# Query-key projection of a linear-attention and feed-forward block: seven block products per pair of tiles, with new engine orders

## The reference

```python
B, N, C, H = 8, 1024, 256, 16          # D = C // H = 16
xn = layernorm(x)                       # x: (8, 1024, 256) float32
qkv = xn @ qkv_w + qkv_b                # to (3, B, H, N, D)
q, k = l2norm(q), l2norm(k)             # over D
kv = einsum('bhnd,bhne->bhde', k, v)
attn = einsum('bhnd,bhde->bhne', q, kv).reshape(B, N, C) @ proj_w + proj_b
ffn = relu(xn @ W1 + b1) @ W2 + b2      # 256 -> 1024 -> 256
out = x + attn + ffn
```

## Time and profile before

| what | value |
|---|---|
| device time, three runs | 553.73, 553.97, 554.46 us (median 553.97) |
| span of the profiled execution, first to last instruction | 552.4 us |
| instructions | 8714 |
| TensorE busy, share of the span | 547.7 us, 99% |
| VectorE, ScalarE, GpSimd busy | 398.5, 286.9, 119.4 us |
| clock granted to TensorE | full speed throughout |

### The profile page before, as it was taken

One profiled execution on the slowest core, in us unless ns is written; L12 is line 12 of the kernel. 1 busy time (PEld: TensorE's weight loads), 2 busy tenths in 40 slices (PEclk: granted clock), 3 DMA queues, 4 the chain that ended last, 5 costly groups with the idle time before them and its releaser, 6 DMA issues.

```text
span 552.4 us, 8714 instructions
## 1 busy us (share of the span) xinstructions
PE 547.7 (99%) x2590; PEld 460.2 (83%) x2590; DVE 398.5 (72%) x791; ACT 286.9 (52%) x529; POOL 119.4 (22%) x150
## 2 busy tenths in 40 slices
PE   9999999999999999999999999999999999999997
PEld 7888888888888888888888888888888888888896
DVE  6977788567795876858667587775777767684655
ACT  4785654556336563465644556455553655533421
POOL 4242424202052020420213202331024201050100
PEclk9999999999999999999999999999999999999999
DMA  8522134343413434134341343315333251314312
GB/s 259 167 87 50 33 83 93 83 105 83 107 20 86 98 85 95 24 86 98 85 88 31 93 92 84 81 38 113 71 90 67 45 107 38 79 37 93 96 39 76
DMA packets 141413, 45.34 MB, mean 82 GB/s; under 512 B 133330, under 2 KB 136402, under 8 KB 141396
## 3 DMA queue, kind: packets, MB, share of 16 engines
q1 hardware_dynamic: 139280, 44.61, 34.7%
q10 hardware_dynamic: 2116, 0.53, 0.5%
HBM read 20.98 MB, written 8.39 MB: 53 GB/s over the span
## 4 chain that ended last, share of the span: by engine, by line
PE 99%; DVE 0%; issue 0%
PE o_bank L1169 12%; PE o_bank L1170 12%; PE o_bank L1171 12%; PE w_bank L1169 11%; PE w_bank L1170 11%; PE w_bank L1171 11%; PE v_bank L1169 7%; PE v_bank L1170 7%; PE v_bank L1171 7%; PE kv_bank L1307 3%; PE g_bank L1307 3%; PE kv_bank L1312 1%; PE g_bank L1312 1%; PE kv_bank L1323 1%; PE w_bank L1361 1%; PE g_bank L1171 0%
## 5 line engine op out<-in xcount | busy, mean ns | idle before, releaser
L957 DVE SCALAR_TENSOR_TENSOR h_lo<-w_bank,h_hi 128x512 fp32r<-128x512 f32 x128 | 87.4, 683 | 38.2 <-ACT h_hi L607 36.5
L607 ACT ACTIVATE h_hi<-w_bank 128x512 fp32r<-128x512 f32 x128 | 76.4, 597 | 66.5 <-PE w_bank L1171 66.4
L1169 PE MATMUL w_bank<-xT_hi,w_hi 128*128 128x512 f32 x254 | 99.9, 393 | 0.0
L1170 PE MATMUL w_bank<-xT_lo,w_hi 128*128 128x512 f32 x254 | 99.2, 391 | 0.0
L1171 PE MATMUL w_bank<-xT_hi,w_lo 128*128 128x512 f32 x254 | 98.9, 389 | 0.0
L1169 PE MATMUL o_bank<-h_hi,w_hi 128*128 128x512 f32 x240 | 93.5, 389 | 0.0
L1170 PE MATMUL o_bank<-h_lo,w_hi 128*128 128x512 f32 x240 | 93.4, 389 | 0.0
L1171 PE MATMUL o_bank<-h_hi,w_lo 128*128 128x512 f32 x240 | 93.4, 389 | 0.0
L405 POOL TENSOR_TENSOR xn_lo<-xn,xn_hi 128x256 fp32r<-128x256 f32 x56 | 42.5, 759 | 217.6 <-ACT xn_hi L517 213.4
L420 POOL TENSOR_TENSOR y_sb<-y_sb,y_rows 128x256 f32<-128x256 f32 x56 | 52.5, 941 | 123.7 <-DVE y_rows L1001 103.2
L585 ACT ACTIVATE qk_sq<-v_bank 128x512 f32<-128x512 f32 x64 | 38.3, 598 | 72.2 <-PE v_bank L1171 72.2
(11 more groups left out here) (213 smaller groups left out, 921.4 us busy)
## 6 DMA issues: line engine op xcount, KB each, us to landing
y_rows<-blocks SPq DMA_DIRECT2D x256, 32.0 KB, 1.9
x_sb<-x SPq DMA_DIRECT2D x15, 512.0 KB, 3.5
y_sb<-x SPq DMA_DIRECT2D x60, 128.0 KB, 3.3
out<-y_sb SPq DMA_DIRECT2D x58, 128.0 KB, 2.5
xT_raw<-blocks SPq DMA_DIRECT2D x224, 32.0 KB, 1.9
y_sb<-w SPq DMA_DIRECT2D x4, 256.0 KB, 5.1
x_sb<-x SPq DMA_DIRECT2D x2, 256.0 KB, 3.0
w_raw<-w SPq DMA_DIRECT2D x2, 256.0 KB, 7.4
```

The source lines that it names most:

```text
L607: nc.scalar.activation(h_hi[:, j % RING, :], w_bank[j % 2][:], ACT.Relu).then_inc(h_done, 1)
L957: nc.vector.scalar_tensor_tensor(h_lo[:, r, :], w_bank[j % 2][:], 0.0, h_hi[:, r, :].bitcast(F32), ALU.max, ALU.subtract).then_inc(h_lo_do ...
L1169: nc.tensor.matmul(to, left[0], right[0], start=first, stop=False, skip_group_check=shared)
L1170: nc.tensor.matmul(to, left[0], right[1], start=False, stop=False, skip_group_check=shared)
```

## The change

For the halves 3 to 15, the 512 x 256 by 256 x 512 query-key product is cut into blocks. A pair `n` (0 or 1) takes tiles `n` and `n + 2` as two block rows, the two channel chunks as the inner blocks, and the query and the key columns of the weight as two block columns. In place of eight block products (24 matmuls of 512 columns per half), seven are computed from sums and differences of blocks: 42 matmuls of 256 columns per half. The sums of the transposed input (`xf_raw`, four forms) are made by GpSimd (`x_forms`, one instruction of 512 elements per partition and two of 256), their high part by ScalarE (`x_forms_high`, 1024 elements) and their low part by VectorE (`x_forms_low`, 1024 elements). The sums of the weights are made once, by GpSimd (`weight_forms`). The shared partial results pass from one quarter of a bank to another between four bursts on TensorE: `qk_begin` (6 narrow matmuls), then ScalarE copies two quarters (`qk_seed`), `qk_second` (6), then VectorE adds (`qk_seed` of VectorE), `qk_third` (6), VectorE adds (`qk_sum`), `qk_fourth` (3). `xf_raw` lies in `xn`, and `wqk_forms` lies in `wvp_raw`, so that `normalise(s)` waits for `x_forms_low(s - 1)` and the first `yT_out(b, 1, ...)` waits for `weight_forms`. The core of the diff:

```diff
+X01_X00, X11_X01, X11_X01_X00, X10_X11_X01_X00 = range(FORMS)
+W_SIX, W_FIVE, W_FOUR, W_SEVEN = range(FORMS)
...
+        xf_raw = xn[:].rearrange("p t c -> p (t c)").rearrange("p (f n) -> p f n", f=FORMS)
+        wqk_forms = wvp_raw[:].rearrange("p w k n -> p (w k n)").rearrange("p (f n) -> p f n", f=FORMS)
...
+        qk_11, qk_22 = (v_bank[0][:, n * C:(n + 1) * C] for n in range(2))
+        qk_12, qk_21 = (v_bank[1][:, n * C:(n + 1) * C] for n in range(2))
...
+    def x_forms(s):
+        wait(pool, x_moved, 16 * MOVES * (s - 1))
+        first, second = slice(0, PAIR * P), slice(PAIR * P, HALF)
+        nc.gpsimd.tensor_tensor(xf_raw[:, 0:2], xT_raw[:, :, second],
+                                xT_raw[:, 0].rearrange("p (a n) -> p a n", a=PAIRS),
+                                ALU.subtract).then_inc(xf_sums_done, 1)
+        wait(pool, xf_sums_done, 2 * (s - FORMS_FROM) + 1)
+        nc.gpsimd.tensor_tensor(xf_raw[:, X11_X01_X00], xT_raw[:, 1, second], xf_raw[:, X01_X00],
+                                ALU.subtract).then_inc(xf_sums_done, 1)
+        wait(pool, xf_sums_done, 2 * (s - FORMS_FROM) + 2)
+        nc.gpsimd.tensor_tensor(xf_raw[:, X10_X11_X01_X00], xT_raw[:, 1, first], xf_raw[:, X11_X01_X00],
+                                ALU.subtract).then_inc(xf_raw_done, 1)
+    def weight_forms():
+        whole = wqk_forms.rearrange("p f n -> p (f n)")
+        pool.wait_ge(wvp_ready, 2)
+        nc.gpsimd.tensor_tensor(whole, wqk_hi[:].rearrange("p k n -> p (k n)").bitcast(F32),
+                                wqk_lo[:].rearrange("p k n -> p (k n)").bitcast(F32),
+                                ALU.add).then_inc(wqk_forms_summed, 1)
+        for n, (to, left, right, op) in enumerate(((W_SEVEN, 3, 1, ALU.add), (W_FIVE, 0, 1, ALU.subtract),
+                                                   (W_SIX, W_SEVEN, 0, ALU.subtract),
+                                                   (W_FOUR, 2, W_SIX, ALU.subtract))):
+            pool.wait_ge(wqk_forms_summed, n + 1)
+            nc.gpsimd.tensor_tensor(wqk_forms[:, to], wqk_forms[:, left], wqk_forms[:, right],
+                                    op).then_inc(wqk_forms_summed, 1)
+        pool.wait_ge(wqk_forms_summed, FORMS + 1)
+        nc.gpsimd.tensor_copy(wqk_forms_hi[:], wqk_forms).then_inc(wqk_forms_hi_ready, 1)
+        pool.wait_ge(wqk_forms_hi_ready, 1)
+        nc.gpsimd.tensor_tensor(wqk_forms_lo[:], wqk_forms, wqk_forms_hi[:].bitcast(F32),
+                                ALU.subtract).then_inc(wqk_forms_ready, 1)
...
+    def x_forms_high(s):
+        wait(act, xf_raw_done, s - FORMS_FROM + 1)
+        copy(xf_hi[:].rearrange("p f (b n) -> p f b n", b=PAIR),
+             xf_raw.rearrange("p f (n b) -> p f b n", b=PAIR)).then_inc(xf_hi_done, 1)
+    def qk_seed(s, n):
+        wait(act, qk_begun, pairs_done(s, n))
+        wait(act, qk_copied, TILES * s + 2 * n)
+        copy(qk_21, qk_11)
+        wait(act, qk_22_summed, pairs_done(s, n) - 1)
+        copy(qk_fifth[:], qk_22).then_inc(qk_seeded, 1)
+    def qk_pair_out(s, u, n, w):
+        if w == 0:
+            wait(act, qk_22_summed, pairs_done(s, n))
+        else:
+            wait(act, qk_21_done, pairs_done(s, n))
+        wait(act, qk_ss_done, TILES * s + 2 * n + w - 1)
+        nc.scalar.activation(qk_sq[:, w, :], v_bank[w][:], ACT.Square).then_inc(qk_sq_done, 1)
+        if n == 0 and w == 0:
+            wait(act, q_transposed, s - 1)
+            wait(act, k_lo_done, s - 1)
+        to = (off_diagonal if w else diagonal)(head_blocks(qk[u]), n)
+        copy(to, v_bank[w][:].rearrange("p (w n) -> p w n", w=2)).then_inc(qk_copied, 1)
...
+    def x_forms_low(s):
+        wait(dve, xf_hi_done, s - FORMS_FROM + 1)
+        less(xf_lo[:].rearrange("p f (b n) -> p f b n", b=PAIR),
+             xf_raw.rearrange("p f (n b) -> p f b n", b=PAIR),
+             xf_hi[:].rearrange("p f (b n) -> p f b n", b=PAIR)).then_inc(xf_lo_done, 1)
+    def qk_seed(s, n):
+        wait(dve, qk_21_sixth_in, pairs_done(s, n))
+        nc.vector.tensor_tensor(qk_12, qk_21, qk_fifth[:], ALU.add).then_inc(qk_12_seeded, 1)
+    def qk_sum(s, n):
+        wait(dve, qk_21_seventh_in, pairs_done(s, n))
+        nc.vector.tensor_tensor(qk_22, qk_21, qk_fifth[:], ALU.add).then_inc(qk_22_summed, 1)
...
+    def qk_begin(s, u, n, batch):
+        if n == 0 and u == 1:
+            wait(pe, yT_added, KC * batch)
+        if n == 0:
+            wait(pe, xT_hi_done, KC * (s + 1))
+            wait(pe, xT_lo_done, KC * (s + 1))
+        wait(pe, qk_copied, TILES * s + 2 * n - 1)
+        product(qk_11, (xT_hi[:, u, 0, tile(n)], xT_lo[:, u, 0, tile(n)]),
+                (wqk_hi[:, 0, 0:C], wqk_lo[:, 0, 0:C]), True, False, shared=True)
+        wait(pe, xf_lo_done, s - FORMS_FROM + 1)
+        qk_form(qk_22, X11_X01, w_form(W_FIVE), n).then_inc(qk_begun, 1)
+    def qk_form(to, x_form, weights, n):
+        hi, lo = weights
+        return product(to, (xf_hi[:, x_form, tile(n)], xf_lo[:, x_form, tile(n)]), (hi, lo), False, False,
+                       shared=True)
...
+    def qk_second(s, u, n):
+        wait(pe, qk_seeded, pairs_done(s, n))
+        qk_form(qk_21, X11_X01_X00, w_form(W_SIX), n).then_inc(qk_21_sixth_in, 1)
+        product(qk_11, (xT_hi[:, u, 1, tile(n)], xT_lo[:, u, 1, tile(n)]),
+                (wqk_hi[:, 1, 0:C], wqk_lo[:, 1, 0:C]), False, True, shared=True)
+    def qk_third(s, n):
+        wait(pe, qk_12_seeded, pairs_done(s, n))
+        qk_form(qk_12, X10_X11_X01_X00, (wqk_hi[:, 1, C:2 * C], wqk_lo[:, 1, C:2 * C]), n)
+        qk_form(qk_21, X01_X00, w_form(W_SEVEN), n).then_inc(qk_21_seventh_in, 1)
+    def qk_fourth(s, u, n):
+        wait(pe, qk_22_summed, pairs_done(s, n))
+        t = PAIR + n
+        product(qk_21, (xT_hi[:, u, 1, tile(t)], xT_lo[:, u, 1, tile(t)]), w_form(W_FOUR), False, True,
+                shared=True).then_inc(qk_21_done, 1)
```

More of the change, by code:

```diff
@@ L1080, in opening @@
                 divide(1, 1, k_done)
-            def half(b, s, u, last):
[L1083 to L1115, removed]
-                else:
[L1117 to L1136, removed]
-                if is_second(s):
-                    qT_low(s, u)
-                if ahead:
-                    h_low(s + 1, 1)
-                    divide(1, 1 - u, k_done)
-                else:
-                    qT_low(s, u)
@@ new lines, in second_half @@
+            def second_half():
+                variance(3, 1, 1)
+                divide(0, 1, q_done)
+                spread(3)
+                k_low(1, 1)
+                transpose_q(1, 1)
+                h_low(1, 3)
+                h_low(1, 4)
+                g_low(0)
+                transpose_x(3)
+                h_low(1, 5)
+                sum_squares(2, 0)
+                h_low(1, 6)
+                sum_squares(2, 1)
+                qT_low(0, 0)
+                sum_squares(2, 2)
+                mask_kv(0)
+                h_low(1, 7)
+                sum_squares(2, 3)
+                bound(2)
+                h_low(2, 0)
+                m_low(0)
+                h_low(2, 1)
+                norms(2)
+                qT_low(1, 1)
+                divide(1, 0, k_done)
@@ new lines, in odd_half @@
+            def odd_half(b, s):
+                divide(0, 1, q_done)
+                transpose_q(s, 1)
+                h_low(s, 2)
+                k_low(s, 1)
+                x_forms_low(s + 1)
+                h_low(s, 3)
+                xT_low(s + 1, 0)
+                variance(s + 2, b + 1, 1)
+                g_low(b)
+                h_low(s, 4)
+                qk_seed(s + 1, 0)
+                spread(s + 2)
+                h_low(s, 5)
+                qk_sum(s + 1, 0)
+                transpose_x(s + 2)
+                mask_kv(b)
+                qk_seed(s + 1, 1)
+                h_low(s, 6)
+                qk_sum(s + 1, 1)
+                sum_pair_squares(s + 1, 0, 0)
+                h_low(s, 7)
+                sum_pair_squares(s + 1, 0, 1)
+                m_low(b)
+                qT_low(s, 1)
+                sum_pair_squares(s + 1, 1, 0)
+                h_low(s + 1, 0)
+                sum_pair_squares(s + 1, 1, 1)
+                bound(s + 1)
+                norms(s + 1)
+                h_low(s + 1, 1)
+                divide(1, 0, k_done)
@@ new lines, in last_odd_half @@
+            def last_odd_half(b, s):
+                h_low(s, 2)
+                divide(0, 1, q_done)
+                h_low(s, 3)
+                transpose_q(s, 1)
+                k_low(s, 1)
+                g_low(b)
+                h_low(s, 4)
+                mask_kv(b)
+                h_low(s, 5)
+                h_low(s, 6)
+                m_low(b)
+                h_low(s, 7)
+                qT_low(s, 1)
+            def half(b, s, u, last):
+                if last:
+                    if u == 0:
+                        last_even_half(b, s)
+                    else:
+                        last_odd_half(b, s)
+                elif is_second(s):
```

(5 more changed lines are left out.)

438 lines of the change are left out of this document (356 added, 82 removed).

## The result

The changed kernel takes 555.09 us (median of 13 runs, 554.55 to 555.33), the kernel before 553.97 us beside it (13 runs, 553.73 to 554.46). The ratio is 1.0019, 95% interval 1.0011 to 1.0027: slower by 1.1 us, at the edge of what I had called the same. I had forecast 551.8.

What follows compares the result with a forecast made beforehand. The prediction took TensorE, busy the whole time, to bound the kernel. TensorE -3.5, the second half +0.7 and loop waits +0.6 gave -2.2 us, so 554.0 became 551.8 us, range 548.5 to 556.8.

Steps and rivals of the forecast that it cites:

- TensorE's stream: Query-key matmuls of 13 halves: -5.7 us, less 2.2 for 74 narrow bursts, so -3.5, at best -5.7.
- short bursts are free: Rival: narrow bursts on TensorE cost nothing extra and nothing waits; 548.6 us, chance 0.16.
- The Trainium skill's figure: Estimate from the skill's matmul formula: 0.6 us won per half, 7.8 in all; not used in the sum.
- The waits in the loop: TensorE waiting for late answers: 0.1 us per odd half, none in even ones; 0.6 in all, between 0 and 3.9.
- GpSimd beside VectorE: Instructions in the loop hold each other: at most 0.76 us each, giving 0 to 0.3 of wait per odd half.
- the opening: The second half, run once before the loop's batches: 0.7 us late, between 0 and 2.
- The even half: Even halves of the loop: answers to TensorE come in time, nothing charged, though 0 to 0.3 us of wait was possible.
- The second half: Run once: `gather` waits for `k_low`, which stands behind `variance`, `divide` and `spread`; 0.7 us, between 0 and 2.
- The waits eat the gain: Rival: 0.2 us of wait in each of 13 halves, 2 in the second half; 554.1 us, chance 0.14.
- the forms come too late: Rival: the chain from `transpose_x` to `begin0` is 0.6 us later per half, 7.8 in all; 559.0 us, chance 0.25.
- the likeliest case: Whole kernel: the forecast itself, faster at 551.8 us (549.8 to 552.8 by its bounds), chance 0.45.
- the slow rival: The chain of forms before `begin0` holds up each half by 0.6 us more; 559.0 us, chance 0.25.

Runs made afterwards that it cites:

- e1: The changed kernel with `h_low2` ahead of `transpose_q` in the odd half: 551.84 us, ratio 0.9964 to the kernel before.
- b1: The changed kernel with e1 and e2 together and the three 1024-element `weight_forms` instructions as four of 256 each: 550.91 us, ratio 0.9945.
- n1: The kernel before with each 512-column query-key product made as two of 256, nothing saved: 559.97 us, ratio 1.0107.
- e2: The changed kernel with GpSimd's first form instruction (512 elements) made as two of 256: 551.96 us, ratio 0.9964.
- e3: The changed kernel with the odd half's form instructions held until its second divide is done, size kept: 553.63 us, ratio 0.9993.
- d1: The changed kernel with the first form instruction doubled to 1024 elements and a wait of GpSimd for `split_xn` added: 559.32 us, ratio 1.0096.
- e4: The changed kernel with VectorE's `m_low(0)` ahead of `bound(2)` in the second half: 554.56 us, ratio 1.0011.

## Why the prediction was wrong, by its own steps

- **TensorE's stream: right, within 0.2.** I had -0.44 per half and 0.03 per burst, -3.5 in all. The bursts run at 0.119; the six wide matmuls behind each take 1.39, and three narrow ones suffice for it, as this row pair behind a `fourth` shows (306.62 to 308.01):

```profile
306.62 0.40 PE L1453 MATMUL w_bank<-xT_hi,w_hi 128*128 128x512 f32 x1
...
308.01 0.28 PE L1453 MATMUL v_bank<-wqk_hi,xT_hi 128*128 128x256 f32 x1
```

  In e1, where nothing waits in the loop, a batch is 66.59: 0.52 less than before, where my sum has 2 x 0.44 - 11 x 0.03 = 0.55. Six batches are 3.1, and the last stretch is shorter than that of before by 0.2 (b1) to 0.4 (the changed kernel). Together -3.3 to -3.5. The rival "short bursts are free" is refuted, by these rows and by n1.
- **The Trainium skill's figure.** The estimate from the Trainium skill (TensorE: Matmul & The Clock Gate, "Back-to-back issue gap"), 0.6 us won per half, is not what the runs show: e1 won 0.26 per half, the price of the bursts included. The section calls the formula one for an isolated matmul; in the streams here the spacings were 0.119 and 0.227, and the measurement decides.
- **The waits in the loop: the step that failed.** I put them at 0.1 for each odd half, 0.6 us in all. They are 0.50 each in the gap and 0.57 each by the batch length against e1: 3.4 in all. The mechanism was named in "GpSimd beside VectorE", with the place and the size both wrong. I had the first form instruction begin at t = 2.1, and looked for the damage at `begin0` and `up6`. In the trace (t = 0 at 318.77) the moves have landed by 1.46, where GpSimd begins, and the second divide could begin at 1.53. These two lie within 0.1 us of each other in every batch, and the divide, which lost, waited 1.1. I had given a two-operand instruction "at most 0.76" in the even half and never asked what the 1.31 us instruction would do to a divide in the odd one; and `down2`, which waits for `h_low2` behind that divide, is in no list of tight places in the prediction. e1 and e2 each remove the whole of it, e3 shows the other winner, d1 shows both. The Trainium skill has the rule that I did not apply (SBUF — State Buffer, "Who interferes with whom"): it calls the ports that VectorE and GpSimd share an exclusive lock, lets a VectorE instruction with two SBUF inputs contend with a GpSimd instruction that reads SBUF, and has the issue order decide which of the two blocks. The trace agrees: 1.31 us of GpSimd, 1.10 of it paid by the divide.
- **The terms, with what was measured.** TensorE -3.5 as forecast, 1.3 in place of 0.7 for the opening, 3.4 in place of 0.6 for the waits: +1.2, and the spans say +1.2.
- **The even half: right.** No gap there; the divide beside `add_rows` takes 1.61 for 1.22 and `xT_low` 1.82, both inside the margins.
- **The second half: size near, reason wrong.** The `gather` does not wait for `k_low`. 0.98 us are lost before `attend`, by `bound` behind a 2.40 us instruction. I had looked only at `mask_kv` for such a hold, so the near size is luck. Batch 0 ends 1.34 later in the profiled runs; 0.14 of it is there already at the first `gather`. The start before the first `attend` differs between profiled runs by up to 0.5 us (the last matmul ahead of it starts at 80.33 to 80.80 in the five kernels that are alike up to there), so the opening's remainder is not settled.
- **The rivals.** "The waits eat the gain" (554.1) is what happened, with one wait of 0.5 per batch in place of 0.2 per half, so that rival had the cause right and the size nearly; "the forms come too late" did not happen in the changed kernel, but did in e3 and d1. The time lies inside the range, which was wide; the likeliest case and the direction were wrong. The range's upper end, 556.8, does not follow from its own words: half of the slow rival's 5.0 above 554.0 is 556.5. Nothing hangs on the difference.

Not tried: the new orders without the seven products. How much of them was needed is therefore open.

## What to carry to other kernels

When two engines share a path, cost a meeting by the length of the longest single instruction on the other side and ask who comes first; if a tenth of a microsecond decides it, count the loss in full, or cut the instruction so that either order is harmless. Narrower matmuls carry their own price, so measure it before counting a saved block product: here narrowness took about 4.9 us of the 8.9 that three of 24 wide matmuls in each of 13 halves are worth. List for every step of a bounding engine the one operand that it takes, with its margin, also where the list of the other engine was not changed at that place.

## What the runs showed of the hardware

- The length and the order of single instructions decide. The `divide` here, a VectorE instruction with two SBUF operands, makes no progress while a GpSimd addition or subtraction is under way, and the reverse (where one hands over to the other the records overlap by up to 0.2 us): a GpSimd instruction of 1.31 us (512 elements) gave a divide pair of 3.46 instead of 2.36; as two of 256 elements it gave 2.90; with 1024 elements it gave 4.61 or, where the divide was first, a GpSimd instruction of 3.46 instead of 2.4. VectorE instructions with one operand in a bank were not held: `m_low` took 0.69 us in the middle of a GpSimd instruction of 2.40 (e4).
- It is not only for two operands: a `tensor_scalar` of 128 float32 elements with one operand took 2.24 us, or 1.02 when it began later (e4), and ended both times 0.08 to 0.09 us after the GpSimd instruction of 2.40; beside a GpSimd copy of 256 elements it took 0.26 (b1). The Trainium skill (SBUF — State Buffer, "Who interferes with whom") lists `tensor_scalar` among the instructions that can take the shared ports in a 2-port mode; the profile does not show the mode, only the hold.
- The wide matmuls behind a narrow burst are slower by about 0.03 us in all (1.39 us for six instead of 1.36), and a burst of three is enough for it.
- After the wait of 0.50 us most of TensorE's next ten wide matmuls started 0.23 to 0.24 us apart in place of 0.227, 0.04 more in sum (the changed kernel against e1).
